# The last stage on GpSimd tile by tile, new orders of work, and the 42-row piece of the down projection as one matmul per tile

## The reference, cut to what matters

```python
xn   = layernorm(x)
q, k, v = split(xn @ Wqkv + bqkv)
qp, kp  = elu(q) + 1, elu(k) + 1
kv   = kp^T @ v          (per batch of 2048 rows);  ksum = sum of kp
attn = (qp @ kv) / (qp . ksum + 1e-6)
z    = layernorm(xn + attn) * g1 + b1
h    = silu(z @ Wg + bg) * (z @ Wu + bu)          # 682 hidden units
s    = layernorm(z + h @ Wd + bd) * g2 + b2
out  = x + s * silu(xn @ ternary(W)^T)
```

## Time and profile before

| | us |
|---|---|
| median of 3 runs | 1376.93 (1376.89 to 1380.07) |
| profiled execution, its own time | 1378.72 |
| its span, first to last instruction | 1376.9 |
| mean granted clock of TensorE | 0.988 of full speed |
| PE busy | 1294.2 (94%) |
| DVE busy | 1118.1 (81%) |
| ACT busy | 994.0 (72%) |
| POOL busy | 665.6 (48%) |

### The profile page before, as it was taken

One profiled execution on the slowest core, in us unless ns is written; L12 is line 12 of the kernel. 1 busy time (PEld: TensorE's weight loads), 2 busy tenths in 40 slices (PEclk: granted clock), 3 DMA queues, 4 the chain that ended last, 5 costly groups with the idle time before them and its releaser, 6 DMA issues.

```text
span 1376.9 us, 24851 instructions
## 1 busy us (share of the span) xinstructions
PE 1294.2 (94%) x8147; PEld 1159.6 (84%) x8147; DVE 1118.1 (81%) x2679; ACT 994.0 (72%) x1750; POOL 665.6 (48%) x462
## 2 busy tenths in 40 slices
PE   7889999999999999999999999999999999999996
PEld 5679888988888988888988889888889888888885
DVE  7987888788888888888888888878988888766665
ACT  5697777777777777678776778677777777766662
POOL 4632543555534555445455445455444554444445
PEclk9999999999999999999999999999999999999999
DMA  6200100111101111101111011111011110011100
GB/s 189 77 17 16 47 17 31 47 47 47 47 1 46 47 47 46 35 14 47 47 47 47 5 43 47 47 46 45 3 46 47 47 32 24 8 32 48 46 16 31
DMA packets 57892, 55.78 MB, mean 41 GB/s; under 512 B 5967, under 2 KB 56997, under 8 KB 57766
## 3 DMA queue, kind: packets, MB, share of 16 engines
...
...
## 4 chain that ended last, share of the span: by engine, by line
PE 69%; DVE 24%; issue 4%; POOL 2%; ACT 1%; DMA 0%; DVEq 0%; SPq 0%; ACTq 0%; POOLq 0%
PE bank L974 44%; PE d_bank L974 16%; DVE xn L733 9%; PE xk_bank L974 6%; PE bank L988 4%; DVE st L707 2%; DVE rz L790 2%; DVE bank L818 2%; DVE h_l L828 2%; DVE kp L760 1%; DVE kp_l L766 1%; DVE den L787 1%; DVE rz L835 1%; DVE den L784 0%; ACT h_h L519 0%
## 5 line engine op out<-in xcount | busy, mean ns | idle before, releaser
L974 PE MATMUL bank<-zT_h,wgu_h 128*128 128x512 f32 x704 | 286.6, 407 | 53.9 <-DVE h_l L828 53.9
L436 POOL TENSOR_TENSOR rstd<-ve,neg_half 128x4 f32<-128x4 f32 x96 | 99.9, 1047 | 465.9 <-DVE ve L718 465.4
L974 PE MATMUL bank<-zT_h,wgu_l 128*128 128x512 f32 x704 | 281.4, 400 | 0.0
L974 PE MATMUL bank<-zT_l,wgu_h 128*128 128x512 f32 x704 | 281.1, 399 | 0.0
L974 PEld LDWEIGHTS bank<-zT_h,wgu_h 128*128 128x128 f32 x704 | 134.2, 191 | 83.1 <-DVE h_l L828 59.0
L828 DVE TENSOR_TENSOR h_l<-bank,h_h 128x512 fp32r<-128x512 f32 x160 | 110.0, 688 | 107.2 <-ACT h_h L519 106.6
L974 PE MATMUL d_bank<-wd_h,h_h 128*128 128x256 f32 x640 | 183.0, 286 | 2.1 <-DVE h_l L828 2.1
L974 PE MATMUL d_bank<-wd_l,h_h 128*128 128x256 f32 x640 | 180.5, 282 | 0.0
L974 PE MATMUL d_bank<-wd_h,h_l 128*128 128x256 f32 x640 | 180.3, 282 | 0.0
L519 ACT ACTIVATE h_h<-bank 128x512 fp32r<-128x512 f32 x160 | 94.8, 593 | 102.0 <-PE d_bank L974 55.2
L974 PEld LDWEIGHTS bank<-zT_l,wgu_h 128*128 128x128 f32 x704 | 134.4, 191 | 32.5
...
## 6 DMA issues: line engine op xcount, KB each, us to landing
...
```

The costliest lines, as they stand in the source:

```text
L436: eng.tensor_tensor(dst, ve[:, k, :], neg_half[:, 0:1].to_broadcast([P, TILES]), ALU.pow).then_inc(S[f"rs{k}"], 1)
L974: ins = eng.matmul(dst, left, right, start=first and n == 0, stop=last and n == len(pairs) - 1, **kw)
```

## The change

The last stage on POOL is cut from four instructions over four tiles into sixteen over one tile each (`last_gain`, `last_offset`, `last_gate`, `last_add`); so is `z_g1`. The semaphores count tiles. The steady orders of all four engines are new. For the 42-unit piece, ten of its units are computed three times over (the projections now have 62 rows, `TH`), and the high and low parts of h and of Wd are laid out over the 128 rows of one operand, with masks (`less_h`, `less_w`) that make of each row a high or a low part, so that all three products of a tile come out of one matmul. POOL copies the high rows of h into rows 0 to 63 of `ht` (`tail_again`), and D 5 waits for that. The weight loads at the start are more in number (vectors 11 to 15, gate and up 4 to 10, down 5 to 11), and POOL makes the masks.

```diff
-    N 2, B 1, N 3, G 3, D 0, U 3, G 4, XK 0, TX 0, U 4, XK 1, TX 1, XK 2, XK 3, GU 5, D 1, D 2,
-    TZ 0, D 3, TZ 1""")
+    N 2, B 1, N 3, G 3, D 0, D 1, U 3, G 4, XK 0, TX 0, U 4, XK 1, TX 1, XK 2, XK 3, GU 5, D 2, TZ 0,
+    D 3, TZ 1""")
 SCALAR_STEPS = steps("""
-    zT_high 0, zT_high 1, xk_copy 0, q_exp 0, q_exp 1, q_high 0, kv_high 0, k_exp 0, kv_high 1,
-    k_exp 1, q_high 1, k_exp 2, silu_gate 0, x_res 0, silu_gate 1, h_high 0, k_high 0, x_res 1,
-    h_high 1, silu_gate 2, silu_tern 0, last_rows 0, last_rows 1, x_res 2, last_rows 2, last_rows 3,
-    k_exp 3, k_high 1, x_res 3, h_high 2, k_high 2, silu_tern 1, silu_gate 3, k_high 3, silu_gate 4,
-    xT_high 0, h_high 3, z_rows 0, z_rows 1, xT_high 1, z_rows 2, z_rows 3, h_high 4, xn_high 0,
-    silu_gate 5, xn_high 1, h_high 5""")
+    zT_high 0, zT_high 1, xk_copy 0, q_exp 0, q_exp 1, kv_high 0, k_exp 0, q_high 0, kv_high 1, k_exp 1,
+    q_high 1, k_exp 2, silu_gate 0, silu_gate 1, x_res 0, h_high 0, h_high 1, last_rows 0, last_rows 1,
+    last_rows 2, silu_gate 2, x_res 1, silu_tern 0, k_high 0, x_res 2, k_high 1, silu_tern 1, k_high 2,
+    h_high 2, x_res 3, k_exp 3, silu_gate 3, k_high 3, last_rows 3, xT_high 0, h_high 3, silu_gate 4,
+    xT_high 1, z_rows 0, z_rows 1, silu_gate 5, z_rows 2, z_rows 3, h_high 4, xn_high 0, h_high 5,
+    xn_high 1""")
 VECTOR_STEPS = steps("""
-    a_stats 0, zT_low 0, zT_low 1, q_elu 0, kv_bias 0, k_add 0, k_add 1, q_elu 1, kv_bias 1,
-    kv_low 0, k_add 2, k_max 0, ffn_rows 0, k_max 1, kv_low 1, ffn_rows 1, q_low 0, ffn_rows 2,
-    ffn_rows 3, q_low 1, k_add 3, last_stats 0, h_rows 0, h_rows 1, h_low 0, last_shift 0, h_low 1,
-    attn 0, attn 1, k_low 0, k_max 2, h_rows 2, a_norm 0, h_low 2, attn 2, k_low 1, attn 3,
-    q_aggregate 0, k_max 3, k_low 2, k_low 3, h_rows 3, attn_norm 0, h_low 3, xT_low 0, h_rows 4,
-    xT_low 1, h_low 4, h_rows 5, h_low 5""")
+    a_stats 0, zT_low 0, zT_low 1, q_elu 0, kv_bias 0, k_add 0, q_elu 1, kv_bias 1, k_add 1, kv_low 0,
+    ffn_rows 0, k_max 0, kv_low 1, k_add 2, ffn_rows 1, ffn_rows 2, q_low 0, q_low 1, ffn_rows 3,
+    k_add 3, k_max 1, last_stats 0, h_rows 0, h_rows 1, h_low 0, last_shift 0, k_max 2, h_low 1, attn 0,
+    attn 1, k_low 0, h_rows 2, k_low 1, attn 2, h_low 2, attn 3, a_norm 0, k_max 3, k_low 2,
+    q_aggregate 0, h_rows 3, k_low 3, attn_norm 0, h_low 3, h_rows 4, xT_low 0, h_rows 5, h_low 4,
+    xT_low 1, h_low 5""")
 GPSIMD_STEPS = steps("""
-    xn_low 0, z_g1 0, xn_low 1, last_rstd 0, a_rstd 0, sum_k 0, last_wide 0, last_wide 1, q_rstd 0,
-    last_wide 2, sum_k 1, last_wide 3, sum_k 2, sum_k 3""")
+    xn_low 0, z_g1 0, z_g1 1, a_rstd 0, z_g1 2, xn_low 1, z_g1 3, sum_k 0, last_rstd 0, last_gain 0,
+    last_gain 1, sum_k 1, last_offset 0, last_offset 1, sum_k 2, last_gain 2, last_gate 0, sum_k 3,
+    last_add 0, last_gate 1, q_rstd 0, last_offset 2, last_gate 2, last_add 1, last_add 2, last_gain 3,
+    last_offset 3, last_gate 3, last_add 3, tail_again 0, tail_again 1""")
...
 END_GPSIMD = steps("""
-    z_g1 0, end_terms 0, last_rstd 0, last_wide 0, last_wide 1, last_wide 2, last_wide 3""")
+    z_g1 0, z_g1 1, z_g1 2, z_g1 3, end_terms 0, last_rstd 0, last_gain 0, last_offset 0, last_gate 0,
+    last_add 0, ...                       # the same four for tiles 1, 2, 3
+    tail_again 0, tail_again 1""")
...
-            eng.dma_start(raw_tail[:, :, 0:HT], rows(wg[:, HF * P:H])).then_inc(s_w["gu"], 16)
-            eng.dma_start(raw_tail[:, :, UT:UT + HT], rows(wu[:, HF * P:H])).then_inc(s_w["gu"], 16)
+            for at, w in ((0, wg), (UT, wu)):
+                eng.dma_start(raw_tail[:, :, at:at + MAIN], rows(w[:, HF * P:HF * P + MAIN])).then_inc(s_w["gu"], 16)
+                for to in range(at + MAIN, at + TH, REM):
+                    eng.dma_start(raw_tail[:, :, to:to + REM], rows(w[:, HF * P + MAIN:H])).then_inc(s_w["gu"], 16)
...
-            def last_wide(g, n):
-                rows = rz[:, g % RZ, :, :]
-                ...
-                    eng.tensor_tensor(rows, rows, each_tile(g2b), ALU.mult).then_inc(S["a"], 1)
+            def last_gain(g, t):
+                if g < GROUPS - 1:
+                    row_ = rz[:, g % RZ, t, :]
+                    eng.wait_ge(S["n2"], TILES * g + t + 1)
+                    eng.tensor_tensor(row_, row_, g2b[:, :], ALU.mult).then_inc(S["a"], 1)
...
+            def tail_again(g, n):
+                eng.wait_ge(S["h"], HC * (g + 1))
+                if g:
+                    eng.wait_ge(S["D"], HC * g)
+                if n:
+                    eng.wait_ge(S["ha"], 2 * g + 1)
+                eng.tensor_copy(ht[n * MAIN:(n + 1) * MAIN, :], hs[0:MAIN, (HC * g + HF) % 2, :]).then_inc(S["ha"], 1)
+                if n:
+                    eng.wait_ge(S["ha"], 2 * (g + 1))
...
             def h_low(g, c):
...
+                    part = ht[UT:UT + TH, :]
+                    eng.scalar_tensor_tensor(out=part, in0=part.bitcast(f32), scalar=less_h[UT:UT + TH, 0:1],
+                                             in1=hidden(g, c)[0:TH, :], op0=ALU.mult, op1=ALU.add)\
+                       .then_inc(S["hl"], 1)
...
+                if c == HF:
+                    eng.wait_ge(S["ha"], 2 * (g + 1))
...
-                        pairs = ((ht[:, s], wd_h[:, c, :]), (ht[:, s], wd_l[:, c, :]))
+                        pairs = ((ht[:, s], wd_h[:, c, :]),)
```

More of the change, by code:

```diff
@@ L38 @@
 UT = 64
+MAIN = 32
+REM = HT - MAIN
+TH = MAIN + 3 * REM
+BIAS = UT + TH
 BATCH, SEQ = 8, 2048
@@ L105 @@
 END_GPSIMD = steps("""
-    z_g1 0, end_terms 0, last_rstd 0, last_wide 0, last_wide 1, last_wide 2, last_wide 3""")
+    z_g1 0, z_g1 1, z_g1 2, z_g1 3, end_terms 0, last_rstd 0, last_gain 0, last_offset 0, last_gate 0,
+    last_add 0, last_gain 1, last_offset 1, last_gate 1, last_add 1, last_gain 2, last_offset 2,
+    last_gate 2, last_add 2, last_gain 3, last_offset 3, last_gate 3, last_add 3, tail_again 0,
+    tail_again 1""")
 DRAIN_VECTOR = steps("""
@@ L117 @@
 FILL_VECTOR = steps("""
-    a_stats 0, k_add 0, k_add 1, k_add 2, k_max 0, setup_gu_low_0 2, setup_ternary 3, setup_bq 2,
+    a_stats 0, k_add 0, k_add 1, k_add 2, k_max 0, setup_d_bias 1, setup_gu_low_0 2, setup_ternary 3, setup_bq 2,
     k_add 3, k_low 0, k_max 1, a_norm 0, k_max 2, k_max 3, k_low 1, k_low 2, xT_low 0, k_low 3,
@@ L151, in schedule @@
     return jobs
-VECTORS = 11
+VECTORS = 15
+GU_LOADS = 10
+D_LOADS = 11
 ITERATIONS = range(-LEAD, GROUPS + 1)
@@ L395, in _ @@
                 if 0 <= last < GROUPS - 1:
-                    eng.wait_ge(S["o"], last + 1)
+                    eng.wait_ge(S["o"], TILES * (last + 1))
                     eng.dma_start(out_v[last], rz[:, last % RZ, :, :]).then_inc(s_out[last % RZ], 16)
@@ L424, in _ @@
                               base=0, pattern=[[-1, P]], channel_multiplier=1).then_inc(s_cst, 1)
+            for n, (mask, tests, rows_) in enumerate((
+                    (less_w, ((ALU.is_ge, BIAS - REM, 1), (ALU.not_equal, BIAS, 1)), slice(MAIN, UT)),
+                    (less_h, ((ALU.is_ge, BIAS - 2 * REM, 1), (ALU.is_ge, BIAS - REM - 1, -1)), slice(UT, UT + MAIN)))):
+                if n:
+                    eng.wait_ge(s_mask, 4 * n)
+                eng.memset(mask[:, :], -1.0).then_inc(s_mask, 1)
+                for k, (op, at, way) in enumerate(tests):
+                    eng.wait_ge(s_mask, 4 * n + k + 1)
+                    eng.affine_select(out=mask[:, :], in_=mask[:, :], compare_op=op, fill=0.0, base=-way * at,
+                                      pattern=[[0, 1]], channel_multiplier=way).then_inc(s_mask, 1)
+                eng.wait_ge(s_mask, 4 * n + 3)
+                eng.memset(mask[rows_, :], -1.0).then_inc(s_mask, 1)
+            eng.wait_ge(s_mask, 8)
             def rstd(k, g, dst):
@@ L508, in _ @@
                 run_steps(order_of(i, FILL_GPSIMD, GPSIMD_STEPS, END_GPSIMD), {
-                    "xn_low": (a, xn_low), "sum_k": (a, sum_k), "z_g1": (f, z_g1), "last_wide": (last, last_wide),
+                    "xn_low": (a, xn_low), "sum_k": (a, sum_k), "z_g1": (f, z_g1), "tail_again": (f, tail_again), "last_gain": (last, last_gain), "last_offset": (last, last_offset),
+                    "last_gate": (last, last_gate), "last_add": (last, last_add),
                     "end_terms": (f, end_terms),
@@ L595, in silu_gate @@
             def silu_gate(g, c):
-                n, rows = HC * g + c, P if c < HF else HT
+                n, rows = HC * g + c, P if c < HF else TH
                 if c < HF:
@@ L622, in h_high @@
                         eng.wait_ge(S["D"], HC * g)
-                    dst = ht[0:rows, :]
+                    dst = ht[UT:UT + rows, :]
                 act(dst, hidden(g, c)[0:rows, :], ACT.Copy, "hh")
@@ L924, in setup_hidden_biases @@
                                   cols(hb0)[:, :, 0:HF], ALU.add).then_inc(S["w_hb"], 1)
[L925 to L926 removed]
+                eng.tensor_tensor(cols(hb)[0:TH, :, HF:HC], cols(hb1)[0:TH, :, HF:HC],
```

(1 more changed line is left out.)

114 lines of the change are left out of this document (66 added, 48 removed).

## The result

| | before | after |
|---|---|---|
| median of the runs on one chip, us | 1378.19 (1376.89 to 1380.07, 4 runs) | 1301.6 (1300.77 to 1301.72, 4 runs) |
| ratio, 95% interval | 1 | 0.9442 (0.9426 to 0.9458) |
| span of the profiled execution | 1376.9 | 1299.1 |
| mean granted clock | 0.988 | 0.993 |

What follows compares the result with a forecast made beforehand. PE bounds the kernel (busy 94%), its steady idle time nearly all 25 waits at U 3 for `h_low 2`. -57.8 - 13.6 + 2.5 - 8.0 + 3.5 + 0.5 = -72.9 us, from 1376.93 to 1304 us; range 1297 to 1312.

Steps and rivals of the forecast that it cites:

- Part 1: Orders of PE and DVE: `h_low 2` ahead of `a_norm`, U 3 behind D 1, removes 2.31 us 25 times: -57.8 us.
- Part 2: D 5 on PE: eight matmuls become four, 0.48 us each iteration, N 0 the thin place: -13.6 us.
- Part 3: POOL's wide instructions cut into tiles: no term of its own, new collisions and thin places +2.5 us.
- Part 4: PE's clock: the five drops in `KV` iterations go once the stall there is gone: -8.0 us.
- Part 5: The fill: 16 more DMAs on SP's queue delay the third group's load and statistics: +3.5 us.
- Part 6: The end, iteration 31: four `z_g1` on POOL add 0.5 us, the copies +0.1: +0.5 us.
- (a): Rival: the clock still falls in the `KV` iterations, 1312 us; chance 0.17.
- (b): Rival: part is given back at N 0, where `h_low 0` comes 0.7 us late, 1322 us; chance 0.15.
- (c): Rival: POOL's new order delays `attn_norm` and `h_low 3`, PE stalls at GU 5, 1390 us; chance 0.03.

Runs made afterwards that it cites:

- e1: Kernel before with only `h_low 2` moved ahead of `a_norm` in DVE's order: 1354.8 us, 0.9823.
- e3: Kernel after with the one matmul per tile of the 42-unit piece (D 5) issued twice: 1315.12 us, 0.9537.
- e11: Kernel before with only `a_norm` moved behind `attn 3` in DVE's order, POOL wide as before: 1332.94 us, 0.9665.
- e2: Kernel before with only the last stage and `z_g1` cut into one instruction per tile, old orders kept: 1338.51 us, 0.9704.
- e4: Kernel after with POOL's last stage wide again, behind `q_rstd`; `z_g1` stays by tiles: 1306.63 us, 0.9471.
- e10: Kernel after with `a_norm` put back directly behind `h_rows 2` on DVE: 1303.0 us, 0.9444.
- e6: Kernel before with `h_low 2` ahead of `a_norm` only in the iterations with `KV`: 1377.57 us, 0.9992.
- e9: Kernel after with `last_rstd` and `tail_again` earlier on POOL, the third group's load ahead of Wd's, and `setup_d_low` cut into five: 1293.45 us, 0.9379.
- e7: Kernel after with `last_rstd` ahead of `end_terms` and `tail_again` ahead of the last tile on POOL: 1299.85 us, 0.9422.
- e5: Kernel before with `h_low 2` ahead of `a_norm` only in the iterations without `KV`: 1362.5 us, 0.9882.

## Why the prediction was right, and which steps were not

**Part 1 (-57.8): right, a little small.** U 3 starts 2.32 us sooner behind the job ahead of it, 25 times. Beside this the matmul that starts after a wait holds its successor for 0.34 us instead of 0.23 (e1's rows: 806.51, then 806.85), another 0.1 each time. By plain iterations: 40.96 - 38.09 = 2.87, less 0.47 for D 5 (e3), is 2.40, and 25 x 2.40 = 60.0. I laid `h_low 2` out with 1.9 us to spare; it has 1.76. But "it doesn't hang on POOL" was not so: `k_low 1` was held for 0.6 us by a tile of POOL. After the result I took the place of `h_low 2` ahead of `a_norm` for the cause, and e1 refuted that. The prediction's own list (`k_low 1`, `attn 2`, `h_low 2`, then `attn 3` and only then `a_norm`) was the right one. e11 shows that `a_norm` behind `attn 3`, without anything else, takes both stalls away and leaves a third. But the prediction gave the whole 57.8 us to the orders and none to the tiles, and the runs don't split it so. Alone, each takes away a part (e11, e2); taken back alone from the kernel after, the wide last stage costs the stretch nothing (e4) and the early `a_norm` 0.9 us (e10). Each covers for the other, with D 1 ahead of U 3 in both runs. The kernel after with both taken back wasn't run. One sum of this part doesn't come out: it puts TX 0 about 7 us behind D 0's end, but its terms give 4.9, and 4.95 is what the profile shows (769.05 to 774.00). `a_norm` ends at 771.25, so nothing hung on it.

**Part 2 (-13.6): right.** D 5 is four matmuls:

```profile
751.09 0.65 PE L1041 MATMUL d_bank<-wd_h,ht 128*128 128x256 f32 x4
```

e3 prices it at 12.3 us in the stretch and 0.7 in the iterations 27 to 30. The thin place was N 0: I put it at 15.6 us into the iteration and the end of `h_low 0` at 15.4; they came at 15.61 and 15.35. For the end I wrote 0.5 and got nothing, as D 5 waits there for POOL's copies, 0.7 us.

**Part 3 (+2.5): nothing of it came.** PE is busy for all of the 1002.51 us. POOL's instructions were sized well (0.74 for a tile; 24.94 us an iteration, forecast 25.1). DVE is busy for 30.87 us, not 29.7: it isn't freed as much as I thought, because it meets POOL more often. In iteration 17 `k_low 0` took 0.86 us and `k_low 1` 0.99 (0.41 when alone), `attn_norm` 0.69 (0.15), and the step that writes `ht` 1.32 (0.75). The Trainium skill ("SBUF — State Buffer", section "Who interferes with whom") says that a DVE instruction with two SBUF inputs contends with a GpSimd instruction that reads SBUF. The rows agree: `k_low 1`, with two such inputs, took 0.99 us beside L502 (0.41 elsewhere), and `h_low`, with one input in a bank, 0.67 as ever. By that rule I had reckoned 3.7 us for DVE, to be taken up by its slack, and left it out of the 29.7; about 1.2 us an iteration beyond that figure came, and slack took it.

**Part 4 (-8.0): the size is right, the reason wrong.** No drop is left in the stretch, and the five `KV` iterations that had one are shorter by 1.6 us each beyond the stall. But I tied the drops to `KV` iterations with a stall. e6 refutes it: there the plain ones have them. (The prediction also counts 25 waits without `KV`; there are 19, and six with it.) In every kernel that no longer has the waits of 2.2 us in the stretch (the one after, e1, e2, e11) the drops there are gone too.

**Part 5 (+3.5): +1.0 in the profile, and that low by chance.** The statistics of the third group start at 30.11, forecast 29; the issue at 23.50, forecast 24.6. Iteration -4 is 3.85 us longer for it, and the next 2.6 us shorter for the race of e9. The others add up to nothing only by chance: +0.9 up to iteration -4, +0.8 in -2, -1.4 in -1 (where the kernel before has its clock at 1.2 GHz for 6.8 us), and -0.5 in 0, which is D 5. In the profiles of e3, e7 and e4, where the race was lost, iteration 1 starts 3.3, 3.4 and 5.6 us later than before; in e10, where it was lost too, 2.2. The term was a fair one for the profiles in which it is lost. I had not seen the race in the profile before: a `k_low` of 3.16 us in the fill, beside POOL's widest instruction.

**Part 6 (+0.5): too small, +1.8.** Iteration 31 takes 1.7 us more, about what one clock drop costs (1.6). The wait at D 0 was 2.10 without a drop and is 2.73 with one. D 0 itself starts only 0.14 us later in the iteration (11.90, 11.76 before), so the four `z_g1` add less than the 0.5 I gave them; the wait is longer since PE gets there sooner. I had left the clock out of this part. That the longer wait brought the drop is not shown: e5 has the old wait of 2.10 us there and a drop, e3 one of 2.25 and none.

Term by term, the spans give -60.0 (Part 1), -12.9 (Part 2: 12.2 in the stretch, 0.7 behind it), 0, -7.8, +1.0 and +1.9, which is the -77.8 measured, where I had -72.9. So the errors of Parts 1, 3 and 5 all point the same way, 7 us together, and Parts 2, 4 and 6 take 2.3 of it back; the medians, which differ by 76.6, hide part of it. Of the rivals, (a) and (b) stayed out, (c) too: GU 5 starts 0.12 us behind XK 3 in the kernel after. Its mechanism, `attn_norm` late and `h_low 3` behind it, is the one that e11 shows, with 0.75 us.
